# Layer gather in the second order: the table's part for a batch is copied to a fixed place by GpSimd

## The chip, the cores and the metric

The kernel runs on one core of a Trainium2 chip. The metric is the device time of one execution in microseconds; several executions give a median.

## What is computed

Four graph layers over 12500 nodes of 128 features and 200000 edges, each with layer norm before and a residual after. Two of their steps matter here, one of layer 2 and one of layer 3:

```python
# layer 2, the second of its two sums over edges
agg_bwd = jax.ops.segment_sum(w[:, None] * x[row], col, num_segments=n)
# layer 3
msg = edge_attr[:, None] * node[src]
ssum = jax.ops.segment_sum(msg, dst, num_segments=n)
```

Both need, for every edge, the row of a table of nodes that the edge's source names, and both add these rows up by the edge's target. The other steps (layer 0's multilayer net, layer 1's attention, layer 2's other sum, the sorting of the edges by source) are not touched by the change.

## The kernel before

The kernel is a row of phases (the loop at line 2767), with a barrier of all engines between any two. `p_lists` to `p_post` sort the edges and write lists; `p_l0` to `p_l1_nodes` are the first two layers; `p_l2f`, `p_l2b`, `p_l2_nodes`, `p_l3`, `p_l3_nodes` are the last two.

The edges stand in two orders. The first goes by target. The second goes by source: the table's 12500 rows are cut into 98 windows of 128, and the edges into NBQ = 558 batches of 512 places each, such that all places of a batch take rows of one window. `produce_q(table)` (line 2309) writes, for each batch, the 512 rows of the table to `xbuf`; `aggregate` then gathers from `xbuf` in the first order and sums. `produce_q` is called twice, by `p_l2b` (table t3d) and by `p_l3` (table t4d). `produce_p` (line 2429) is its sister for the other direction: 482 batches, four to a piece of the table, which GpSimd splits into three parts (lines 2478 to 2484 and 2520) at fixed places. It is not changed.

In `produce_q` the engines share a batch b like this:

- Before the batches, ScalarE (line 2365) and VectorE (line 2386) turn the whole table, in groups of four windows, into three bfloat16 parts whose sum is the float32 value. They lie in `TAB`, 384 elements (3 parts of 128) a window. The semaphore `pc[2]` says that all groups are there.
- ScalarE fetches the list `rowsqd` (which row of the window each place takes), half a round of six batches at a time (line 2353).
- TensorE spreads a batch's 512 row numbers to all 128 partitions with one product into PSUM bank s % 3 (line 2405, `kb`). It does so for batch b + 2 ahead of the products of batch b.
- VectorE compares them with the partition's number: 0 and 1 in bfloat16, 128x512 (line 2395, `oh`), in one of three places.
- TensorE makes 12 products (line 2419): four blocks of 128 places by three parts, summed in PSUM bank 3 + s % 3 (`gm`). The part of the table is read at `TAB` from an address in a register.
- ScalarE copies the bank to one of six places of `OUT` (line 2373, `ev`), and SyncE stores it to `xbuf`, 256 KB (line 2343).

The batches run in rounds of UN = 6: the first and the last round are written out, the 91 between them are a loop on each engine (`peeled`, line 2292). NITQ = 93 is the number of rounds. At the head of every round TensorE's queue loads the addresses of the round's six windows from the tile `RNG` (row 96) into registers, by `ranges` (line 153). `p_bases` (line 709) had written them as the window's number times 384. `past` (line 2303) is the wait that keeps a writer from a place still in use; in a loop it computes the semaphore's value in a register.

Of the kernel before, what the change touches and what calls it, by code (L numbers as in the profile page):

```python
# [5 lines left out]
I32 = mybir.dt.int32  # L6
U32 = mybir.dt.uint32
BF16 = mybir.dt.bfloat16
ALU = mybir.AluOpType
# [4 lines left out]
BE = 512  # L14
TP = 80
UN = 6
# [8 lines left out]
def gnn(nc, x, src, dst, ea, ew, u, W1, b1, W2, b2, w, w_r, att, loop_w, Ws, bs, Wd, bd_,  # L25
# [22 lines left out]
    NITQ = (((NE + 3 * NCK * NW) // 4 + 127 * NW + 127) // 128 + UN - 1) // UN  # L48
    NBQ = NITQ * UN
# [22 lines left out]
    NC = max(NN + 132, 12632)  # L72
    AREA = sb("AREA", [128, 3 * NC])
# [8 lines left out]
    RNG = sb("RNG", [128, max(2 * NR, 8 * NCK, 2 * NBQ) + 2], I32)  # L82
# [70 lines left out]
    def ranges(e, part, col, n, top_=None):  # L153
        return nc.values_load_multi_w_load_instructions(
            RNG[32 * part:32 * part + 1, bass.ds(col, n)], engines=[e.engine], min_val=0, max_val=top_ or NN + 1,
            skip_runtime_bounds_check_because="keys are node numbers")[1]
# [484 lines left out]
    def p_bases():  # L641

        p = Phase()
        n = NCK
        LOWF, IOX = p.tile([128, 128]), p.tile([128, NBQ])
# [19 lines left out]
        @p.on("vector")  # L665
        def _(e):
            link = chain(e, dv)
            e.wait_ge(ld, 16)
            e.wait_ge(g, 3)
            link(e.memset(ONS[:], 1.0))  # L670
            link(e.tensor_tensor_scan(LBI[0:n], ONS[0:n], NGR[0:n], 0.0, ALU.mult, ALU.add))
            e.memset(LBG[:, 98:99], -1.0)
            link(e.tensor_tensor(LBG[0:n, 0:98], LBI[0:n], NGR[0:n], ALU.subtract))
            e.wait_ge(mm, 2)
            link(e.tensor_scalar(CTI[:], PS[:, 4, 0:98], 127.0, None, ALU.add))
            e.tensor_copy(PRE[0:n], PS[0:n, 5, 0:98])
            link(e.tensor_scalar(CTI[:], CTI[:], 7, None, ALU.arith_shift_right))
            link(e.tensor_copy(TB[:], CTI[:]))
            link(e.tensor_tensor_scan(TBI[:], ONS[:], TB[:], 0.0, ALU.mult, ALU.add))
            link(e.tensor_tensor(TB[:], TBI[:], TB[:], ALU.subtract))  # L680
            link(e.scalar_tensor_tensor(out=DQ[0:n], in0=TB[0:n], scalar=128.0, in1=PRE[0:n], op0=ALU.mult, op1=ALU.add))
            link(e.tensor_tensor(DQ[0:n], DQ[0:n], LBG[0:n, 0:98], ALU.subtract))
            e.tensor_copy(DD[0:n, 0:1], DQ[0:n, 0:1])
            e.tensor_copy(DD[0:n, 98:99], DQ[0:n, 97:98])
            link(e.tensor_tensor(DD[0:n, 1:98], DQ[0:n, 1:98], DQ[0:n, 0:97], ALU.subtract))
            e.nop().then_inc(mm, 1)
            e.wait_ge(mm, 4)
            e.tensor_scalar(LBT[0:99, :], PS[0:99, 4, 0:n], -1.0, 0.5, ALU.mult, ALU.add)
            e.tensor_copy(TBT[0:98], PS[0:98, 6, 0:1])
            link(e.tensor_copy(DT[0:99], PS[0:99, 5, 0:n]))  # L690
            d3 = DD3.rearrange("p (k t) -> p t k", t=3) if (3 * NCK) % 2 == 0 else DD3[:, 0:3 * NCK].rearrange("p (k t) -> p t k", t=3)
            link(e.tensor_copy(d3[0:99, 0, :], DT[0:99]))
            link(e.tensor_tensor(DR[0][0:99], DT[0:99], d3[0:99, 0, :], ALU.subtract))
            link(e.tensor_copy(d3[0:99, 1, :], DR[0][0:99]))
            link(e.tensor_tensor(DR[1][0:99], DR[0][0:99], d3[0:99, 1, :], ALU.subtract))
            e.tensor_copy(d3[0:99, 2, :], DR[1][0:99])
            link(e.tensor_scalar(WG[0:98], IOX[0:98], TBT[0:98, 0:1], None, ALU.is_ge))
            e.nop().then_inc(mm, 1)
            e.wait_ge(mm, 6)


            for q in range(0, NBQ, 512):
                m = min(512, NBQ - q)
                i = e.tensor_scalar(IOX[:, q:q + m], PS[:, 6 + q // 512, 0:m], float(NW - 1), None, ALU.min)
            link(i)
            o = RNG[64:65, 0:2 * NBQ].rearrange("o (b t) -> o b t", t=2)
            e.tensor_scalar(o[:, :, 0], IOX[64:65, :], 128.0, None, ALU.mult)
            e.tensor_scalar(o[:, :, 1], IOX[64:65, :], 128.0, 1.0, ALU.mult, ALU.add)
            link(e.tensor_scalar(RNG[96:97, 0:NBQ], IOX[96:97, :], 384.0, None, ALU.mult))

        @p.on("tensor")
        def _(e):
# [1579 lines left out]
    def peeled(e, nb, un, f):  # L2292

        n = nb // un
        for b in range(un):
            f(b, b, 0)
        with e.Fori(1, n - 1) as it:
            for s in range(un):
                f(it * un + s, s, it)
        for b in range(un * (n - 1), nb):  # L2300
            f(b, b % un, b // un)

    def past(e, sem, b, back, each=1):

        n = b + 1 - back
        if not isinstance(n, int) or n > 0:
            e.wait_ge(sem, n * each)

    def produce_q(table):


        p = Phase()
        A0 = NC
        TAB = AREA[:, A0:A0 + 192 * 98].bitcast(BF16)
# [4 lines left out]

        RWZ = AREA[:, A0:A0 + UN * BE // 2]  # L2320
        RW = RWZ.bitcast(BF16).rearrange("o (s k) -> o s k", s=UN)
        OUT = [GF[:, 512 * s:512 * s + 512] for s in range(UN)]
        STG = [XR[:, 512 * i:512 * i + 512].rearrange("n (w f) -> n w f", w=4) for i in range(4)]
        groups = [(w_, min(4, NW - w_)) for w_ in range(0, NW, 4)]
        tl, fr = [p.sem(f"tl{i}") for i in range(4)], p.sem("fr")
        pc, sb_ = [p.sem(f"pc{i}") for i in range(3)], [p.sem(f"sb{i}") for i in range(2)]
        ra, rb, kb, oh, gm, ev, rz = (p.sem(k) for k in ("ra", "rb", "kb", "oh", "gm", "ev", "rz"))
# [5 lines left out]
        @p.on("sync")  # L2333
        def _(e):
            for k, (w_, m) in enumerate(groups):
                if k >= 4:
                    e.wait_ge(pc[2], k - 3)
                e.dma_start(STG[k % 4][:, 0:m, :], table[128 * w_:128 * (w_ + m), :].rearrange("(w n) f -> n w f", n=128)
                            ).then_inc(tl[k % 4], 16)

            def step(b, s, it):
                e.wait_ge(ev, b + 1)
                e.dma_start(xv[bass.ds(b, 1)].rearrange("b p k -> (b p) k"), OUT[s]).then_inc(st[s], 16)
            peeled(e, NBQ, UN, step)
            for s in range(UN):
                e.wait_ge(st[s], 16 * NITQ)

        @p.on("scalar")
        def _(e):
# [26 lines left out]
                    rows(it + 1, s // H)  # L2376
            peeled(e, NBQ, UN, step)

        @p.on("vector")
        def _(e):  # L2380
            def rest(k, i):
                if 0 <= k < len(groups):
                    w_, m = groups[k]
                    e.wait_ge(pc[i], k + 1)
                    v = STG[k % 4][:, 0:m, :]
                    e.tensor_tensor(v, v, tv[:, w_:w_ + m, i, :], ALU.subtract).then_inc(sb_[i], 1)
            e.memset(RWZ, 0.0).then_inc(rz, 1)
            for k in range(len(groups) + 1):
                rest(k, 0)
                rest(k - 1, 1)  # L2390

            def step(b, s, it):
                e.wait_ge(kb, b + 1)
                past(e, gm, b, 3)
                e.tensor_scalar(OHT[s % 3], PS[:, s % 3, :], IP[:, 0:1], None, ALU.is_equal).then_inc(oh, 1)  # L2395
            peeled(e, NBQ, UN, step)

        @p.on("tensor")
        def _(e):
            e.wait_ge(pc[2], len(groups))  # L2400

            def spread(b, s, it):
                e.wait_ge((ra, rb)[s // H], it * 16 + 16)
                past(e, oh, b, 3)
                e.matmul(PS[:, s % 3, :], ONB[:], RW[:, s, :], start=True, stop=True).then_inc(kb, 1)  # L2405
            held = {}

            def step(b, s, it):
                if s == 0:
                    held[0] = ranges(e, 3, it * UN, UN, 384 * 97)  # L2410
                if s + 2 < UN:
                    spread(b + 2, s + 2, it)
                elif not (isinstance(it, int) and it == NITQ - 1):
                    spread(b + 2, s + 2 - UN, it + 1)
                e.wait_ge(oh, b + 1)
                past(e, ev, b, 3)
                for r in range(4):
                    for k in range(3):
                        i = e.matmul(PS[:, 3 + s % 3, 128 * r:128 * r + 128], OHT[s % 3][:, 128 * r:128 * r + 128],  # L2419
                                     TAB[:, bass.ds(held[0][s] + 128 * k, 128)], start=(k == 0), stop=(k == 2))  # L2420
                i.then_inc(gm, 1)
            spread(0, 0, 0)
            spread(1, 1, 0)
            peeled(e, NBQ, UN, step)
# [371 lines left out]
```

## Time and profile before

| what | value |
| --- | --- |
| median of 3 runs | 9346.08 us |
| lowest, highest | 9331.73, 9353.26 us |
| the profiled execution's own time | 9342.07 us |
| its span | 9340.4 us |
| mean granted TensorE clock | 0.881 |
| PE busy | 7261.6 us (78%) |
| VectorE (DVE) busy | 6413.4 us (69%) |
| GpSimd (POOL) busy | 4037.3 us (43%) |
| ScalarE (ACT) busy | 3252.4 us (35%) |

PE is TensorE's matmul, PEld its weight load, SP is SyncE; a q behind an engine's name is its sequencer. Times stand in microseconds from the start of the span unless marked ns. A row of instructions gives the source line, the engine, the operation, what it writes and reads, how many there are, and their shortest, median and longest duration in ns. A row of the timeline gives the start, the length and then the instructions merged in it; in brackets is how long the engine had been idle, and what ended that. "issue" is time in which the engine waited for nothing that the profile shows. Granted clock is a share of TensorE's full speed, which is 2.4 GHz.

### The profile page before, as it was taken

The numbers are of one execution on the slowest core, as the hardware profiler recorded it, in microseconds if no ns is written. First come the engines' busy times: TensorE is split into PE (matmuls) and PEld (weight loads), VectorE is DVE, ScalarE is ACT, GpSimd is POOL, SyncE is SP. The second block draws the span as 40 slices with busy tenths as digits, with TensorE's granted clock in tenths as the row PEclk, the third lists the DMA queues.
The fourth block names the chain that finished last, engine by engine and source line by source line (L and its number), as shares of the span: only waits on it lengthen the run. The fifth ranks groups of instructions, "written<-read, shape, count | busy, mean of one in ns | idle before, by whom it ended". The sixth has DMA issues, their size and how long they took to land. (4 is left out here: it accounts for less than half of the span.)

```text
span 9340.4 us, 229910 instructions
## 1 busy us (share of the span) xinstructions
PE 7261.6 (78%) x60542; PEld 5838.2 (63%) x60851; DVE 6413.4 (69%) x20871; ACT 3252.4 (35%) x9379; POOL 4037.3 (43%) x4385
## 2 busy tenths in 40 slices
PE   4855677899968888888868977758877775886777
PEld 4855566544446666666667766646666664666665
DVE  5999888511167777777777766656666676666667
ACT  3533322222223333333235500025520025557882
POOL 2000577000057777777625567730037740006771
PEclk7975789999977777777789999989999988999997
DMA  0000466300024444444347866665556644556663
GB/s 21 2 2 1 110 140 140 91 24 24 23 73 105 107 105 106 106 105 105 91 147 271 289 183 191 191 156 230 230 199 191 192 156 178 230 230 183 184 182 106
DMA packets 645062, 1262.07 MB, mean 135 GB/s; under 512 B 126526, under 2 KB 183433, under 8 KB 644569
## 3 DMA queue, kind: packets, MB, share of 16 engines
q1 hardware_dynamic: 424337, 704.50, 23.0%
q0 software_dynamic: 199040, 544.46, 21.7%
q10 hardware_dynamic: 21452, 10.20, 0.4%
q8 instruction: 124, 2.03, 0.1%
q14 instruction: 109, 0.89, 0.0%
HBM read 780.96 MB, written 477.75 MB: 135 GB/s over the span
## 5 line engine op out<-in xcount | busy, mean ns | idle before, releaser
L1063 PE MATMUL PS<-w,GS 128*128 128x128 f32 x12176 | 1641.7, 284 | 499.9 <-DVE AREA L1008 224.2
L1063 PEld LDWEIGHTS PS<-w,GS 128*128 128x128 f32 x12176 | 1459.6, 192 | 682.3 <-DVE w L967 437.6
L1188 POOL DMA_INDIRECT GS<-xbuf,KI x964 | 1031.2, 1070 | 1759.7 <-ACTq L132 710.1
L1171 POOL DMA_INDIRECT GS<-t1d,KI x1564 | 1493.6, 955 | 488.0 <-issue 459.6
L2395 DVE TENSOR_SCALAR AREA<-PS,IP 128x512 bf16<-128x512 f32 x1116 | 837.7, 751 | 439.6 <-PE PS L2405 361.1
L967 DVE TENSOR_TENSOR w<-IO,KI 128x512 f32<-128x512 f32 (+1 forms) x1355 | 808.6, 597 | 424.6 <-issue 413.4
L2419 PE MATMUL PS<-AREA 128*128 x13392 | 961.1, 220 | 11.1 <-ACT GS L2373 1.4
L2419 PEld LDWEIGHTS PS<-AREA 128*128 128x128 bf16 x13392 | 843.8, 98 | 170.2 <-issue 49.2
L2373 ACT ACTIVATE GS<-PS 128x512 f32<-128x512 f32 x1116 | 666.3, 597 | 613.8 <-PE PS L2419 613.5
L1188 POOL DMA_INDIRECT GS<-pbuf,XR x558 | 595.3, 1067 | 209.4 <-issue 101.4
L1598 ACT ACTIVATE w<-PS,w 128x48 f32<-128x48 f32 x1564 | 341.7, 301 | 926.9 <-PE PS L1593 926.9
L1126 ACT ACTIVATE GS<-GS,XR 128x128 f32<-128x128 f32 x1928 | 603.6, 389 | 106.0 <-DMA GS<-xbuf,KI 98.3
L1063 PE MATMUL PS<-w,XR 128*128 128x128 f32 x3128 | 510.7, 313 | 165.8 <-DVE w L967 162.3
L2405 PE MATMUL PS<-AREA,ONB 128*128 128x512 bf16 x928 | 353.2, 381 | 340.2 <-issue 143.1
L1650 PE MATMUL PS<-w,XR 128*128 128x128 f32 x3128 | 586.2, 345 | 0.0
L1063 PEld LDWEIGHTS PS<-w,XR 128*128 128x128 f32 x3128 | 430.8, 214 | 205.9 <-DVE w L967 197.1
L1207 POOL DMA_INDIRECT keyd<-AREA x482 | 480.0, 996 | 178.8 <-issue 146.1
L1644 PE MATMUL PS<-w,GS 128*128 128x128 f32 x3128 | 543.2, 332 | 0.0
L1650 PEld LDWEIGHTS PS<-w,XR 128*128 128x128 f32 x3128 | 500.3, 244 | 49.2 <-issue 28.6
L1008 DVE TENSOR_TENSOR AREA<-AREA,PS 128x128 f32 (+1 forms) x1921 | 515.9, 269 | 18.0
L967 DVE TENSOR_TENSOR w<-IO,XR 128x512 f32<-128x512 f32 x558 | 388.6, 696 | 192.5 <-issue 188.3
L1644 PEld LDWEIGHTS PS<-w,GS 128*128 128x128 f32 x3128 | 514.8, 248 | 0.5
(410 smaller groups left out, 12508.2 us busy)
## 6 DMA issues: line engine op xcount, KB each, us to landing
xbuf<-GS SPq DMA_DIRECT2D x1116, 256.0 KB
XR<-in_edge_attr SPq DMA_DIRECT2D x780, 256.0 KB
pbuf<-AREA SPq DMA_DIRECT2D x482, 256.0 KB
GS<-t1d,KI POOLq DMA_INDIRECT x1564
GS<-xbuf,KI POOLq DMA_INDIRECT x964
GS<-pbuf,XR POOLq DMA_INDIRECT x558
AREA<-t2d ACTq DMA_DIRECT2D x121, 64.0 KB
keyd<-AREA POOLq DMA_INDIRECT x482
```

The costliest lines, as they stand in the source:

```text
L967: return e.tensor_tensor(SEL[s % 3], IO[:, 0:width].unsqueeze(1).to_broadcast([128, 4, width]), kl.unsqueeze(2).to_broadcast([128, 4, widt ...
L1008: i = e.tensor_tensor(ACC[:, bass.ds(wv, width)], ACC[:, bass.ds(wv, width)], PS[:, q, 0:width], ALU.add).then_inc(acc, 1)
L1063: i = e.matmul(PS[:, s % 3, 0:128], feats(s)[0:m, r, 0:D], SELW[s % 3][0:m, width * r:width * r + 128], start=(r == 0), stop=(r == 3))
L1126: i = e.activation(feats(s)[:, r, :], feats(s)[:, r, :], ACT.Copy, scale=weight[:, bass.ds(b * 4 + r, 1)])
L1171: e.indirect_dma_start(GS[0:m, s, r, 0:wide], None, table, bass.IndirectOffsetOnAxis(ap=idx[0:m, c:c + 1].bitcast(U32), axis=0)).then_inc( ...
L1188: e.indirect_dma_start(GF[:, 512 * s:512 * s + 512], None, buf, bass.IndirectOffsetOnAxis(ap=idx[:, b:b + 1].bitcast(U32), axis=0)).then_i ...
L1207: e.indirect_dma_start(keyd, bass.IndirectOffsetOnAxis(ap=SI[:, b:b + 1].bitcast(U32), axis=0), MP[:, 5 * b:5 * b + 5], None).then_inc(sc[ ...
L1644: n = e.matmul(PS[:, 4 + i, 0:128], GS[0:m, s, r, 0:D], LLW[l][0:m, WD * r:WD * r + 128], start=(r == 0), stop=(r == 3))
L1650: n = e.matmul(PS[:, 4 + i, 128:256], EA[0:m, s, r, :], LLW[l][0:m, WD * r:WD * r + 128], start=(r == 0), stop=(r == 3))
L2373: e.activation(OUT[s], PS[:, 3 + s % 3, :], ACT.Copy).then_inc(ev, 1)
L2395: e.tensor_scalar(OHT[s % 3], PS[:, s % 3, :], IP[:, 0:1], None, ALU.is_equal).then_inc(oh, 1)
L2419: i = e.matmul(PS[:, 3 + s % 3, 128 * r:128 * r + 128], OHT[s % 3][:, 128 * r:128 * r + 128], TAB[:, bass.ds(held[0][s] + 128 * k, 128)], ...
```

## The change

In `produce_q`, TensorE no longer reads `TAB` at an address from a register. GpSimd, which had nothing to do in these stages, copies the 384 bfloat16 elements of the batch's window to one of six fixed places `WT`, as an integer addition of zero on 192 words of 32 bits; TensorE waits for the copy (`wt`) and reads there. GpSimd waits until the products of six batches earlier are done (`gm`), and loads the addresses of 18 batches at once, in a loop of 18 batches. The addresses are in words of 32 bits now, so the factor in `p_bases` is 192.

```diff
-            link(e.tensor_scalar(RNG[96:97, 0:NBQ], IOX[96:97, :], 384.0, None, ALU.mult))
+            link(e.tensor_scalar(RNG[96:97, 0:NBQ], IOX[96:97, :], 192.0, None, ALU.mult))
...
+        A0 += UN * BE // 2
+
+        WTI = [AREA[:, A0 + 192 * i:A0 + 192 * i + 192].bitcast(I32) for i in range(UN)]
+        WT = [AREA[:, A0 + 192 * i:A0 + 192 * i + 192].bitcast(BF16) for i in range(UN)]
+        TABI = AREA[:, NC:NC + 192 * 98].bitcast(I32)
+        assert A0 + 192 * UN <= 3 * NC and NITQ % 3 == 0
+        ZI = p.tile([128, 1], I32)
+        wt, zi = p.sem("wt"), p.sem("zi")
...
+        @p.on("gpsimd")
+        def _(e):
+
+            e.memset(ZI[:], 0).then_inc(zi, 1)
+            e.wait_ge(zi, 1)
+            e.wait_ge(pc[2], len(groups))
+            held = {}
+
+            def step(b, s, it):
+                if s == 0:
+                    held[0] = ranges(e, 3, it * (3 * UN), 3 * UN, 192 * 97)
+                past(e, gm, b, UN)
+                e.tensor_tensor(WTI[s % UN], TABI[:, bass.ds(held[0][s], 192)], ZI[:, 0:1].to_broadcast([128, 192]),
+                                ALU.add).then_inc(wt, 1)
+            peeled(e, NBQ, 3 * UN, step)
...
-            held = {}
 
             def step(b, s, it):
-                if s == 0:
-                    held[0] = ranges(e, 3, it * UN, UN, 384 * 97)
                 if s + 2 < UN:
                     spread(b + 2, s + 2, it)
                 elif not (isinstance(it, int) and it == NITQ - 1):
                     spread(b + 2, s + 2 - UN, it + 1)
                 e.wait_ge(oh, b + 1)
+                e.wait_ge(wt, b + 1)
                 past(e, ev, b, 3)
                 for r in range(4):
                     for k in range(3):
                         i = e.matmul(PS[:, 3 + s % 3, 128 * r:128 * r + 128], OHT[s % 3][:, 128 * r:128 * r + 128],
-                                     TAB[:, bass.ds(held[0][s] + 128 * k, 128)], start=(k == 0), stop=(k == 2))
+                                     WT[s][:, 128 * k:128 * k + 128], start=(k == 0), stop=(k == 2))
```

## Rows read from the trace of the kernel before

**Rows 1.** Windows: length, busy us of PE, PEld, DVE, ACT, POOL; PEclk, DMA share, GB/s.

```profile
6254.00:6892.00 638.00, 530.27 (x7159) 437.05 (x7251) 418.32 (x558) 332.47 (x557) 0.00 (x0) 1.00 0.59 229
7789.00:8428.00 639.00, 531.21 (x7160) 437.42 (x7252) 418.79 (x558) 332.76 (x558) 0.00 (x0) 1.00 0.59 229
```

**Rows 2.** Who waited for whom, 6254 to 6892: us in total, times, longest.

```profile
ACT GS L2373 <- PE PS L2419: 306.7, 556, 3.1
DVE AREA L2395 <- PE PS L2405: 180.5, 277, 1.9
PEld PS L2405 <- issue: 115.9, 92, 1.9
```

**Rows 3.** Line 154, register loads on TensorE's sequencer, 6262 to 6889.

```profile
L154 PEldq TENSOR_LOAD <-RNG x92: 1040/1576/2093, 6260.7 to 6885.5; - x92
```

**Rows 4.** Timeline of one round, 6504.9 to 6511.

```profile
6505.83 0.10 PEld L2405 LDWEIGHTS PS<-AREA,ONB 128*128 128x128 bf16 x1
...
6506.71 0.10 PEld L2405 LDWEIGHTS PS<-AREA,ONB 128*128 128x128 bf16 x1
...
6507.60 0.10 PEld L2405 LDWEIGHTS PS<-AREA,ONB 128*128 128x128 bf16 x1
...
6508.74 0.60 ACT L2373 ACTIVATE GS<-PS 128x512 f32<-128x512 f32 x1 [0.29 <-PE PS L2419]
6510.23 0.10 PEld L2405 LDWEIGHTS PS<-AREA,ONB 128*128 128x128 bf16 x1 [1.70 <-issue]
```

**Rows 5.** Line 2405's weight loads, first stage, then second.

```profile
L2405 PEld LDWEIGHTS PS<-AREA,ONB x558: 95/98/151, 6252.9 to 6889.7; 128*128 128x128 bf16 x186
...
L2405 PEld LDWEIGHTS PS<-AREA,ONB x558: 95/98/151, 7788.3 to 8425.3; 128*128 128x128 bf16 x186
```

**Rows 6.** produce_p: weight loads in the timeline, then line 2614's waits, 4960 to 5370.

```profile
4952.10 0.10 PEld L2621 LDWEIGHTS PS<-AREA 128*128 128x128 bf16 x1
...
4952.99 0.10 PEld L2621 LDWEIGHTS PS<-AREA 128*128 128x128 bf16 x1
...
4953.88 0.10 PEld L2621 LDWEIGHTS PS<-AREA 128*128 128x128 bf16 x1
...
  POOL AREA L2520: 55.5, 150
```

**Rows 7.** Windows inside produce_p, columns as in rows 1.

```profile
4960.00:5060.00 100.00, 92.31 (x1310) 79.21 (x1335) 77.03 (x104) 55.39 (x103) 52.09 (x129) 1.00 0.82 288
```

**Rows 8.** GpSimd's additions: two of the timeline, then by line.

```profile
4940.04 0.42 POOL L2480 TENSOR_TENSOR AREA<-AREA 128x128 f32<-128x128 f32 x1
4940.54 0.40 POOL L2482 TENSOR_TENSOR AREA<-AREA,w 128x128 bf16<-128x128 f32 x1
...
L2478 POOL TENSOR_TENSOR AREA<-AREA,w x121: 397/398/400, 4909.0 to 5379.3; 128x128 bf16<-128x128 f32 x121
...
L2480 POOL TENSOR_TENSOR AREA<-AREA x121: 425/427/432, 4909.5 to 5379.8; 128x128 f32<-128x128 f32 x121
...
L2238 POOL TENSOR_TENSOR KI<-XR,RDEG x25: 1029/1036/1197, 4676.0 to 4867.6; 128x512 f32<-128x512 f32 x24, 53x512 f32<-53x512 f32 x1
```

**Rows 9.** Register loads elsewhere: GpSimd's one (line 2459), VectorE's, 7000 to 7600.

```profile
L2459 POOLq TENSOR_LOAD <-w x1: 504/504/504, 4906.0 to 4906.0; - x1
...
L154 DVEq TENSOR_LOAD <-RNG x71: 540/849/871, 7001.7 to 7569.0; - x71
```

**Rows 10.** Timeline of the first stage's beginning.

```profile
6252.86 0.13 PEld L2405 LDWEIGHTS PS<-AREA,ONB 128*128 128x128 bf16 x2 [59.43 <-ACT AREA L2365]
...
6254.40 1.24 PEld L2419 LDWEIGHTS PS<-AREA 128*128 128x128 bf16 x12 [0.57 <-issue]
```

**Rows 11.** VectorE's comparison in produce_p: by line, then two in the timeline.

```profile
L2583 DVE TENSOR_SCALAR AREA<-PS,IP x482: 740/751/753, 4909.6 to 5381.3; 128x512 bf16<-128x512 f32 x161
...
4945.91 1.55 DVE L2583 TENSOR_SCALAR AREA<-PS,IP 128x512 bf16<-128x512 f32 x2
```

**Rows 12.** VectorE's comparison in both stages of produce_q.

```profile
L2395 DVE TENSOR_SCALAR AREA<-PS,IP x1116: 740/751/752, 6253.5 to 8425.8; 128x512 bf16<-128x512 f32 x186
```

## The prediction

> **What bounds the kernel now.** I read the stages first. Line 2419's products and line 2405's spreads run in two stretches only, one for each call of produce_q, 6254 to 6892 us and 7789 to 8428 us [rows 1, 5], 638 us each; the rest of the kernel holds none of the edited lines and I leave it alone. In these two stretches no engine is full: PE is busy 83% of the time, VectorE 66%, ScalarE 52%, GpSimd not at all, the transfer engines 0.59 of the time, and PE's granted clock is 1.00, the 2.4 GHz level [rows 1]. So the next thing to read is who waits, and on what: ScalarE and VectorE wait for PE (307 and 181 us), while PE's weight loads wait 116 us for "issue", that is for nothing that the profile shows, in 92 pieces [rows 2]. 92 is one less than the 93 rounds of six batches. The same count has the register load: 92 TENSOR_LOADs of 1.04 to 2.09 us on PE's sequencer [rows 3].
>
> The order in time shows it as a picture [rows 4]. Inside a round the weights of a batch's spread begin to load at 6505.83, 6506.71 and 6507.60: 0.886 us apart (two pitches in 1.77). Then the next one begins at 6510.23, 2.63 us later, with 1.70 us of "issue" before it. PE's sequencer reaches the head of the loop, asks for six addresses, and nothing is sent to the array until they have come. One stage takes (6889.7 - 6252.9)/557 = 1.1433 us a batch by its first and last spread, the other (8425.3 - 7788.3)/557 = 1.1436 [rows 5], against 0.886 within a round: 0.257 us a batch, or 1.54 us a round. The stage is bound by PE plus this hole in it.
>
> **What the change removes.** The load of the registers and the 46 ns address instructions (three a batch) leave PE. Without the hole PE should hold 0.886 us. Does the loop's end cost anything by itself? The trace answers: lines 2621 and 2614 make the same one-hot products, 12 and a spread, with no register load on PE. Line 2621's weight loads begin at 4952.10, 4952.99 and 4953.88 [rows 6], 0.89 and 0.89 us apart, in a stage whose PE loop ends every eight batches; the PE busy share there is 92% at a granted clock of 1.00 [rows 7]. Its remaining idle time is put to GpSimd, 55.5 us in 150 waits [rows 6]. So a denser PE keeps its clock, and 0.886 can be held.
> The saving is 636.8 - 557 x 0.886 = 143.3 us in the first stage and 637.0 - 493.5 = 143.5 us in the second, 286.8 us together.
>
> **What it adds: a GpSimd copy for each batch.** 1116 integer additions of 128x192, of a broadcast zero, and one load of 18 registers for 18 batches. No such form is in the trace, so I bound it. Below: the 128x128 additions of produce_p, 0.40 us with a broadcast operand and 0.43 with two full ones [rows 8]. Above: the 128x512 addition at 1.036 us [rows 8]. The slope between 427 ns and 1036 ns is 1.59 ns an element, which gives 0.43 + 64 x 0.00159 = 0.53 us. I take 0.53, since 192 lies nearest to the 128 row; whether integers cost GpSimd more no row says, and the end at 1.04 stays in the range. Between two additions stand 0.08 us (starts at 4940.04 and 4940.54 for 0.42 of work [rows 8]). The load: one value took GpSimd 0.50 us [rows 9]; VectorE's loads, of two or twelve values, took 0.54 at the least and 0.85 in the middle [rows 9], near 0.03 us a value, so 18 take 1.0 to 1.1. With branch and the last copy under way I put 1.5 us, with 2.1 as the upper end from PE's slowest. Per batch: 0.53 + 0.08 + 1.5/18 = 0.69 us, under PE's 0.886. The work is hidden by PE. The hole at the end of 18 is hidden too: six places let GpSimd be up to six batches ahead, and five finished ones give PE 5 x 0.886 = 4.4 us to live on. If the cover were gone (a copy above 0.72 us), GpSimd would set the pace at once.
>
> The Trainium skill, page "Runtime: NRT & Kernel Launch", section "Instruction fetch mechanics", puts a register load at about 200 ns a register. An estimate by it: 18 x 0.2 = 3.6 us a load, GpSimd at 0.81 us a batch in place of 0.69, still below PE, though a copy of 0.61 us would then be enough to make it the bound. The twelve-value loads of 0.85 us in this trace don't agree with it, and the sum goes by them.
>
> **What it adds as waits.** PE waits for `wt` before each batch's products. Behind that wait stand the following spreads, so a late copy would also starve VectorE; at 0.69 against 0.886 it isn't late after the first batch. At the start of a stage GpSimd loads (1.1) and copies (0.53) after the table is complete. Before, PE's first product came 1.54 us after its first spread (6252.86 and 6254.40) [rows 10]; now 1.6 or a little more: 0.2 us each, below the rounding. GpSimd waits for `gm`, six batches back; nothing is queued behind it but copies. The factor 192 for 384 in p_bases costs nothing, same instruction. The zeroing of ZI is one tiny GpSimd instruction while it is idle.
>
> **What is late next.** VectorE's comparison, 0.751 us, can follow itself at 0.80 (two in 1.55 us) [rows 11], under 0.886. ScalarE's copy takes 0.60 [rows 4]. The stores: 262144 bytes in 0.886 us are 296 GB/s; produce_p moves 288 with engines at 0.82 of the time [rows 7]. If 288 were the most, a batch would take 0.91 us and the gain be 260 us; this sets the upper end of the main case. None of them binds first.
>
> **Sum.** 9342.07 (the profiled execution, span 9340.4) - 286.8 + 0.4 = 9055.7. The median of the three runs, 9346.08, is 4 above the profiled one, so I say 9060.
>
> **Rivals.**
> Main case, PE holds 0.886 in both stages: 9060, its own range 9040 to 9085. Chance 0.80.
> GpSimd becomes the pace, though still better than before. It needs a copy of 0.73 to 0.98 us (0.886 and 1.143 less 0.16 for gap and load). For it: integers have no row. Against: 128x128 at 0.40 [rows 8]. With a copy at 0.85 the pace is 1.01, gain 1116 x 0.133 = 148: about 9200. Chance 0.10.
> GpSimd becomes the pace and the kernel slower. The same place, the copy before each batch's products, from 0.98 us on. Priced with the 512-element row, 1.04 + 0.16 = 1.20 us a batch: 1116 x 0.057 = +64, 9410. Against it: a third of those elements. Chance 0.03.
> GpSimd and VectorE exclude each other. If a comparison could not run beside a copy, a batch would take 0.751 + 0.53 = 1.28 us: 1116 x 0.138 = +154, 9500. Against: in produce_p, with GpSimd busy 52% [rows 7], VectorE's comparison of this very form takes 740/751/753 ns [rows 11] and 740/751/752 where GpSimd is silent [rows 12], and GpSimd's additions vary by 3 ns [rows 8]. Chance 0.03.
> The Trainium skill, page "SBUF — State Buffer", section "SBUF: two separate sides", speaks of such a lock: the pair of ports that VectorE and GpSimd share goes to one instruction whole, and the other blocks, for a VectorE operation in a two-port mode or with two SBUF inputs. Would it hold here, the 9500 above is the time; the comparison reads PSUM, so the rule itself exempts it, and the rows agree.
> The hole stays. If the 2.6 us came from the branch and the round's end and not from the load, nothing is won: 9346. Against: line 2621's unbroken pitch [rows 6] and loads as many as holes [rows 2, 3]. Chance 0.04.
>
> **How the numbers follow.** A measurement of this kernel tells about 0.2% from no change, 19 us. Faster by more: main and the first rival, 0.90. Within: the hole stays, 0.04. Slower: 0.06. The range starts at 9035 (a pitch of 0.87, with the run spread) and goes to 9140 (a pitch of 0.955, into the first rival, copy near 0.80); what is left out is its dearer part and the three others, under 2 in 10.
>
> **What would show it.** Right: line 2405's weight loads 0.886 us apart through all rounds, x558 in 494 us; no register load on PE in these stages; both stages some 495 us long; VectorE near 85% busy, transfers near 0.77 and 296 GB/s; copies of about 0.53 us on GpSimd. ScalarE's waits for PE fall from 307 us to around 160. Wrong: PE's idle time put to the GpSimd copy; copies above 0.72 us; VectorE's comparison or the copies much longer than alone; granted clock under 1.00; or pitch kept at 0.886 with holes remaining every six batches. If the stages lose 143 us each and the total doesn't, something outside of them moved.

## The result, and the profile after

The changed kernel takes 9121.03 us in the median of four runs (9113.24 to 9125.56), the kernel before 9343.43 beside it (9331.73 to 9353.26): ratio 0.9762, 95% interval 0.9745 to 0.9778. It is faster by 222 us, inside the range; 9060 had been said, 283 under the kernel before by these runs. So a good fifth of the gain is missing, 61 us, and the study asks where it stayed.

The two stages have shrunk. Windows of both, with the columns of [rows 1]:

```profile
6244.00:6780.00 536.00, 501.46 (x7254) 430.88 (x7254) 418.96 (x559) 333.90 (x560) 273.62 (x558) 0.99 0.71 274
...
7673.00:8200.00 527.00, 500.62 (x7254) 430.18 (x7254) 418.72 (x558) 333.62 (x560) 274.19 (x558) 0.99 0.72 278
```

They are 102 and 112 us shorter than in [rows 1], where 143 each was the sum. More exact are the spreads (line 2429 now, against [rows 5]), first stage and then second:

```profile
L2429 PEld LDWEIGHTS PS<-AREA,ONB x558: 97/98/152, 6244.8 to 6775.6; 128*128 128x128 bf16 x186
...
L2429 PEld LDWEIGHTS PS<-AREA,ONB x558: 97/98/151, 7673.5 to 8196.3; 128*128 128x128 bf16 x186
```

(6775.6 - 6244.8)/557 = 0.953 us a batch, and 0.939 in the second, not 0.886. From first to last the stages are 106.0 and 114.2 us shorter, 220 of the 225 between the two profiled spans (9340.4 and 9115.2). The excess over 0.886 is 557 x (0.067 + 0.053) = 67 us; 5 of them lie in the slower beginnings, since pad20 below, without holes, has an excess of 5 as well. Now the copy, the load of registers and VectorE's comparison, by line:

```profile
L2399 POOL TENSOR_TENSOR AREA<-AREA,w x1116: 493/504/507, 6246.7 to 8194.0; 128x192 int32<-128x192 int32 x186
...
L154 POOLq TENSOR_LOAD <-RNG x62: 1532/2119/6195, 6244.8 to 8178.2; - x62
...
L2419 DVE TENSOR_SCALAR AREA<-PS,IP x1116: 743/751/752, 6245.4 to 8196.8; 128x512 bf16<-128x512 f32 x186
```

The copy is 0.504 us, close to the 0.53 of the prediction. The comparison is what it was in [rows 12] although GpSimd now works beside it. The load isn't what was reckoned: 1.0 to 1.1 had been put, 2.1 is the median and 6.2 the longest. Who waited for whom, 6245 to 6780, against [rows 2]:

```profile
ACT GS L2381 <- PE PS L2441: 200.6, 556, 4.1
POOL AREA L2399 <- PE PS L2441: 159.3, 344, 2.3
POOL AREA L2399 <- issue: 150.7, 16, 58.4
...
PEld PS L2441 <- issue: 36.7, 19, 2.4
PE PS L2441 <- POOL AREA L2399: 31.8, 16, 2.1
```

TensorE waits 16 times for a copy, 2.0 us each, and GpSimd stands 16 times at "issue" before a copy: once for 58.4 us at the stage's start, and 15 times for 6.2 us. There are 31 loads in a stage, so only every second one shows. The loads one by one bear this out, three that follow each other:

```profile
L154 POOLq TENSOR_LOAD <-RNG x1: 5951/5951/5951, 6294.4 to 6294.4; - x1
L154 POOLq TENSOR_LOAD <-RNG x1: 2111/2111/2111, 6314.3 to 6314.3; - x1
L154 POOLq TENSOR_LOAD <-RNG x1: 5942/5942/5942, 6330.2 to 6330.2; - x1
```

It goes on so, by turns, to the end. What a long one does, in the order of time:

```profile
6294.05 0.50 POOL L2399 TENSOR_TENSOR AREA<-AREA,w 128x192 int32<-128x192 int32 x1 [0.38 <-PE PS L2441]
...
6298.97 0.10 PEld L2429 LDWEIGHTS PS<-AREA,ONB 128*128 128x128 bf16 x1
...
6300.73 1.89 POOL L2399 TENSOR_TENSOR AREA<-AREA,w 128x192 int32<-128x192 int32 x4 [6.17 <-issue]
...
6301.46 0.67 PEld L2441 LDWEIGHTS PS<-AREA 128*128 128x128 bf16 x12 [2.40 <-issue]
...
6302.09 0.10 PEld L2429 LDWEIGHTS PS<-AREA,ONB 128*128 128x128 bf16 x1
```

GpSimd's last copy is at 6294.05, its next at 6300.73. TensorE uses up the five places that lie ready, stands before its products from about 6299, and starts with them when the first new copy is done. Two spreads that should be 0.89 apart are 3.12 apart (6298.97 and 6302.09). In the second stage the long loads take 5.61 us and leave 1.72.

### The profile page after: what moved, and what is told of

The parts are those of the page before. It is cut to its first block and busy times, and to the rows that moved or that the text cites. A ratio compares the mean times of both kernels' runs of the same rounds, so it can differ in the third digit from the quotient of the medians.

```text
span 9115.2 us, 230332 instructions
## 1 busy us (share of the span) xinstructions
PE 7221.3 (79%) x60850; PEld 5827.1 (64%) x60851; DVE 6414.1 (70%) x20871; ACT 3251.0 (36%) x9379; POOL 4580.0 (50%) x5503
## 5 line engine op out<-in xcount | busy, mean ns | idle before, releaser
L1063 PEld LDWEIGHTS PS<-w,GS 128*128 128x128 f32 x12176 | 1457.8, 192 | 678.9 <-DVE w L967 444.5
L2441 PE MATMUL PS<-AREA 128*128 128x128 bf16 x13392 | 934.7, 220 | 56.4 <-POOL AREA L2399 56.4
L2399 POOL TENSOR_TENSOR AREA<-AREA,w 128x192 int32<-128x192 int32 x1116 | 547.8, 504 | 615.7 <-PE PS L2441 330.2
L2429 PE MATMUL PS<-AREA,ONB 128*128 128x512 bf16 x1116 | 425.4, 382 | 137.2 <-ACT AREA L2373 137.2
```

Of the source, the lines that this page charges most:

```text
L1063: i = e.matmul(PS[:, s % 3, 0:128], feats(s)[0:m, r, 0:D], SELW[s % 3][0:m, width * r:width * r + 128], start=(r == 0), stop=(r == 3))
L2399: e.tensor_tensor(WTI[s % UN], TABI[:, bass.ds(held[0][s], 192)], ZI[:, 0:1].to_broadcast([128, 192]), ALU.add).then_inc(wt, 1)
```

## Experiments

Why does every second load take three times as long? The list has one word of 4 bytes for a batch, so the loads of 18 begin 72 bytes apart: every second one begins 8 bytes past a multiple of 16. The kernel before had the same alternation on TensorE, unseen in the prediction: its loads of six, 24 bytes apart, took 1.1 us in even rounds and 2.0 in odd ones, behind one median of 1576 ns in [rows 3]. Two of them that follow each other:

```profile
L154 PEldq TENSOR_LOAD <-RNG x1: 1991/1991/1991, 6508.0 to 6508.0; - x1
L154 PEldq TENSOR_LOAD <-RNG x1: 1142/1142/1142, 6515.3 to 6515.3; - x1
```

Theory: where a load begins sets its time. Rival: a long load leaves GpSimd behind, and that makes the next one short, by turns.

**pad20: every load of 18 begins at a multiple of 16 bytes.**

```diff
-            link(e.tensor_scalar(RNG[96:97, 0:NBQ], IOX[96:97, :], 192.0, None, ALU.mult))
+            q3 = RNG[96:97, 0:0 + 20 * (NBQ // 18)].rearrange("o (g t) -> o g t", t=20)
+            link(e.tensor_scalar(q3[:, :, 0:18], IOX[96:97, :].rearrange("o (g t) -> o g t", t=18), 192.0, None, ALU.mult))
...
-                    held[0] = ranges(e, 3, it * (3 * UN), 3 * UN, 192 * 97)
+                    held[0] = ranges(e, 3, it * 20, 3 * UN, 192 * 97)
```

> The changed kernel, but the addresses of 18 batches lie 20 words apart in the list, so that every one of GpSimd's loads of 18 registers begins at a multiple of 16 bytes (72 bytes apart before: every second one began 8 bytes past such a multiple). Theory (where a load begins sets its time; the changed kernel's loads of 5.6 to 6.0 us are the ones that begin 8 bytes off): all 62 loads take about 2.0 to 2.1 us, TensorE never waits for a copy, the spreads are 0.886 us apart all through, and the 61 us of holes go: 9121 - 61 = 9060 us. Rival (a slow load leaves GpSimd behind, and that makes the next one quick, by turns, wherever they begin): loads still 5.9 and 2.1 by turns, 9121 us.

9068.7 us (five runs) against 9355.02 of the kernel before beside it: ratio 0.9695 (0.9682 to 0.9708), 286.3 us less. The prediction's sum was 286.8 for the holes. By first and last spread the two stages are 281.8 us shorter (496.0 each); the other 4 lie within the interval, so that the two numbers agree to half a microsecond is luck. Loads, then TensorE's one remaining wait for a copy in the first stage, then the stage's window:

```profile
L154 POOLq TENSOR_LOAD <-RNG x62: 1537/1990/2120, 6247.4 to 8122.3; - x62
...
PE PS L2442 <- POOL AREA L2400: 1.2, 1, 1.2
...
6251.00:6743.00 492.00, 487.11 (x7107) 426.32 (x7198) 415.16 (x554) 330.50 (x554) 274.40 (x555) 1.00 0.77 295
```

No load is above 2.12 us, TensorE waits for a copy once (1.2 us), and the transfers run at 295 GB/s. The mean pitch is 0.8905 us by first and last spread, 0.886 from one to the next after the first few. The 61 us are back. It beats both kernels. The alternation is gone, so the rival is out.

**pad20off8: every load begins 8 bytes past a multiple.**

```diff
+            q3 = RNG[96:97, 2:2 + 20 * (NBQ // 18)].rearrange("o (g t) -> o g t", t=20)
...
+                    held[0] = ranges(e, 3, it * 20 + 2, 3 * UN, 192 * 97)
```

> As pad20, but the list begins two words later, so that every load begins 8 bytes past a multiple of 16. Theory: all loads of the loop take 5.6 to 6.0 us, and TensorE has a hole of 1.7 to 2.2 us every 18 batches where the changed kernel has it every 36: 61 us more than the changed kernel, 9180 us. Rival (by turns): 9121 us.

9224.19 us, ratio 0.9865 (0.985 to 0.988). With the data, the order and the number of loads of pad20, only 8 bytes further on, they take:

```profile
L154 POOLq TENSOR_LOAD <-RNG x62: 4048/5630/6496, 6249.2 to 8277.0; - x62
```

5.96 us in the first stage and 5.61 in the second, in every round but the first two of each. So the place where a load begins sets its time. The size of the loss was off: 155 us over pad20, where 122 was forecast. Windows of the first stage, the second, three stretches around one hole of the first, and the 4.1 us behind another of its holes, which ends at 6367.9:

```profile
6256.00:6840.00 584.00, 515.00 (x7089) 445.91 (x7181) 414.39 (x553) 329.62 (x553) 269.71 (x553) 0.95 0.64 248
7752.00:8296.00 544.00, 491.75 (x7097) 424.76 (x7188) 414.89 (x553) 329.75 (x553) 268.27 (x553) 1.00 0.69 267
6500.50:6502.60 2.10, 0.84 (x13) 0.78 (x14) 0.00 (x0) 0.00 (x0) 1.58 (x4) 1.00 0.51 198
6502.60:6506.70 4.10, 3.88 (x39) 3.48 (x38) 2.08 (x3) 1.79 (x3) 2.66 (x6) 0.58 0.33 129
6506.70:6515.00 8.30, 8.25 (x123) 7.12 (x122) 6.92 (x10) 5.38 (x10) 4.54 (x9) 1.00 0.69 267
6368.70:6372.80 4.10, 4.05 (x62) 3.53 (x61) 3.16 (x5) 2.86 (x5) 3.50 (x8) 1.00 0.49 191
```

Behind the hole that ends at 6501.8 the granted clock is 0.58 for 4.1 us, that is mostly at the lower level of 1.2 GHz, and 1.00 after them; behind the other one, as long, it stays at 1.00. It falls behind 17 of the first stage's 30 holes of some 2.2 us, and the spreads behind such a hole lose 1.6 us more. In the second stage, with holes of 1.7 us, it falls behind none of the 30. The spreads give the whole account: the holes cost 119 us, the falls of the clock 27, and the longer first loads 5. That is 152 us over pad20; the medians say 155. The forecast of 122 had left out the clock.

**before_pad8: the same cure for the kernel before.**

```diff
-            link(e.tensor_scalar(RNG[96:97, 0:NBQ], IOX[96:97, :], 384.0, None, ALU.mult))
+            q3 = RNG[96:97, 0:0 + 8 * (NBQ // 6)].rearrange("o (g t) -> o g t", t=8)
+            link(e.tensor_scalar(q3[:, :, 0:6], IOX[96:97, :].rearrange("o (g t) -> o g t", t=6), 384.0, None, ALU.mult))
...
-                    held[0] = ranges(e, 3, it * UN, UN, 384 * 97)
+                    held[0] = ranges(e, 3, it * 8, UN, 384 * 97)
```

> The kernel before, with TensorE's own loads of six registers, but the list has 8 words a round, so that every load begins at a multiple of 16 bytes. In the kernel before the loads took 1.1 us in the even rounds and 2.0 us in the odd ones, which began 8 bytes off. Theory: all loads 1.1 us, the odd rounds' holes shrink by 0.87 us, 93 times over both stages: 81 us less than the kernel before, 9262 us. Rival (by turns): 9343 us, no change.

9272.24 us, ratio 0.991 (0.9895 to 0.9926), 83 us less than the kernel before, as the theory has it. TensorE's loads in the first stage, against [rows 3]:

```profile
L154 PEldq TENSOR_LOAD <-RNG x92: 1022/1111/1257, 6269.0 to 6852.5; - x92
```

**six: GpSimd loads six registers at a time, list as it was.**

```diff
-                    held[0] = ranges(e, 3, it * (3 * UN), 3 * UN, 192 * 97)
+                    held[0] = ranges(e, 3, it * UN, UN, 192 * 97)
...
-            peeled(e, NBQ, 3 * UN, step)
+            peeled(e, NBQ, UN, step)
```

> The changed kernel, but GpSimd loads the addresses of six batches at a time (rounds of 6 in place of 18, the list as it is, 24 bytes apart, every second load 8 bytes off). Theory: a load's time goes with the number of registers and where it begins, some 1.1 us even and 2.0 us odd as on TensorE before; GpSimd's mean is 0.50 + 1.7/6 or so = 0.79 us a batch, still under 0.886, and each load is shorter than the 4.4 us that five finished places cover. TensorE has no hole: 9060 us. If GpSimd's loads of six take over 2.6 us in the mean, it sets the pace and the time goes above 9060 by 1116 us for each us a batch.

9070.51 us, ratio 0.97 (0.9687 to 0.9713). All loads of both stages:

```profile
L154 POOLq TENSOR_LOAD <-RNG x186: 802/1080/1909, 6252.3 to 8137.3; - x186
```

They alternate, 1.02 and 1.85 us, and none reaches what the places cover. Nothing is lost (pad20 took 9068.7): what hurt was not the number of misplaced loads but that one of them was longer than the cover.

**load20: two registers more, an aligned 20.**

```diff
-                    held[0] = ranges(e, 3, it * 20, 3 * UN, 192 * 97)
+                    held[0] = ranges(e, 3, it * 20, 20, 192 * 97)
```

> pad20, but GpSimd loads 20 registers at a time, and uses 18. Theory (a load makes one access of about 0.33 us for each whole, aligned 16 bytes and one for each single word besides: 18 words from an aligned start are 4 + 2 = 6 accesses, 1.98 us; 18 from 8 bytes off are 18 accesses, 5.6 to 5.9): 20 aligned words are 5 accesses, so the load is shorter by one access, about 1.65 us, though it brings two registers more. Rival (an aligned load costs by the register, 0.11 us each): 2.2 us. The time stays that of pad20, 286 us under the kernel before, since the load is covered either way.

One run: 9047.38 us, 284 under its kernel before (9331.69). What the run is read for is not its time but the loads:

```profile
L154 POOLq TENSOR_LOAD <-RNG x62: 1322/1786/1914, 6245.1 to 8117.5; - x62
```

1.91 us in the first stage and 1.75 in the second, where 18 took 2.11 and 1.98. Two registers more make it 0.2 us shorter: the rival by the register is out. A whole access of 0.33 was forecast to go, and 0.2 went, so the size of an access isn't the same throughout.

**before_load8: TensorE loads an aligned eight.**

```diff
-                    held[0] = ranges(e, 3, it * 8, UN, 384 * 97)
+                    held[0] = ranges(e, 3, it * 8, 8, 384 * 97)
```

> before_pad8, but TensorE loads 8 registers a round and uses 6. Theory by accesses: 2 in place of 3, so a load is 0.3 us shorter, 186 holes shrink by that, and the time is some 56 us under before_pad8, 139 under the kernel before. Rival (by the register): loads 0.1 to 0.2 us longer, 20 to 40 us over before_pad8.

9169.56 us, ratio 0.9827 (0.9814 to 0.9841), 162 under the kernel before, that is 79 more than before_pad8 gained; 139 and 56 were forecast. The loads of the first stage:

```profile
L154 PEldq TENSOR_LOAD <-RNG x92: 598/662/846, 6261.4 to 6804.2; - x92
```

0.66 us against 1.11 with six registers. They are 0.45 us shorter, not 0.3, and 186 x 0.45 = 84 us accounts for the gain. The same exchange, one sixteen-byte piece for two single words, saved only 0.2 us on GpSimd (load20); why is open. More than half of the whole gain could thus be had without GpSimd's copies, by the place and length of the loads alone. The rest is about what the loads of 0.66 us still cost on TensorE, 186 x 0.66 = 123 us. The change takes them away by moving them to GpSimd; whether TensorE could hide them by itself, by asking for a round's addresses earlier, was not tried.

**three: three places in place of six.**

```diff
-                past(e, gm, b, UN)
-                e.tensor_tensor(WTI[s % UN], TABI[:, bass.ds(held[0][s], 192)], ZI[:, 0:1].to_broadcast([128, 192]),
+                past(e, gm, b, 3)
+                e.tensor_tensor(WTI[s % 3], TABI[:, bass.ds(held[0][s], 192)], ZI[:, 0:1].to_broadcast([128, 192]),
...
-                                     WT[s][:, 128 * k:128 * k + 128], start=(k == 0), stop=(k == 2))
+                                     WT[s % 3][:, 128 * k:128 * k + 128], start=(k == 0), stop=(k == 2))
```

> pad20 with three places for the copies in place of six: GpSimd can be three batches ahead, not six. Theory (a load is covered by the batches that lie ready, and what is left of it is TensorE's hole; in the changed kernel 5.95 us left 2.22 and 5.61 left 1.72, so six places cover 3.7 to 3.9): three places cover 3 x 0.886 = 2.66 less, 1.1 to 1.2 us, and a load of 1.98 to 2.11 leaves 0.8 to 1.0 us, every 18 batches: 60 holes, 53 us, so 233 under the kernel before. If the number of places did not matter at these loads: 286 under it.

9108.82 us against 9331.69, ratio 0.9762 (0.9748 to 0.9775), 223 less (233 forecast). The hole in the order of time:

```profile
6426.76 0.10 PEld L2430 LDWEIGHTS PS<-AREA,ONB 128*128 128x128 bf16 x1
...
6427.65 0.10 PEld L2430 LDWEIGHTS PS<-AREA,ONB 128*128 128x128 bf16 x1
...
6427.90 0.60 ACT L2382 ACTIVATE GS<-PS 128x512 f32<-128x512 f32 x1 [0.29 <-PE PS L2442]
6428.20 1.43 POOL L2400 TENSOR_TENSOR AREA<-AREA,w 128x192 int32<-128x192 int32 x3 [2.31 <-PE PS L2442]
6428.93 0.67 PEld L2442 LDWEIGHTS PS<-AREA 128*128 128x128 bf16 x12 [1.19 <-ACT GS L2382]
...
6429.56 0.10 PEld L2430 LDWEIGHTS PS<-AREA,ONB 128*128 128x128 bf16 x1
```

A load of 2.1 us, fully hidden with six places, leaves 1.0 us with three (6427.65 to 6429.56, less 0.89). The row puts the wait down to ScalarE, whose copy was done at 6428.5; the first of GpSimd's three ended some 0.2 us later, just ahead of the products. By first and last spread the two stages lose 53.7 us against pad20, where 53 was forecast; the medians differ by 10 more.

**twice: each copy made twice.**

```diff
+        WDI = [AREA[:, A0 + 192 * i:A0 + 192 * i + 192].bitcast(I32) for i in range(UN, 2 * UN)]
...
+                e.tensor_tensor(WDI[s % UN], TABI[:, bass.ds(held[0][s], 192)], ZI[:, 0:1].to_broadcast([128, 192]),
+                                ALU.add).then_inc(wt, 1)
...
-                e.wait_ge(wt, b + 1)
+                e.wait_ge(wt, b * 2 + 2)
```

> pad20, but GpSimd makes each copy twice (once to places that nobody reads). The copies follow each other at 0.462 us when nothing holds them, so a batch takes GpSimd 2 x 0.462 = 0.924 and the load (2.84 - 0.46)/18 = 0.13 more: 1.06 us, over TensorE's 0.886. Theory (from there GpSimd sets the pace): 1116 x 0.17 = 194 us over pad20, some 92 under the kernel before, still faster since 1.143 is the point of return; TensorE waits for the copy in nearly every batch. VectorE's comparison stays at 0.751 us though GpSimd is busy nearly all the time.

9097.85 us against 9331.69, ratio 0.9751 (0.9738 to 0.9765): 234 less than the kernel before, where 92 was forecast. The window inside the first stage, then VectorE's comparison:

```profile
6250.00:6750.00 500.00, 495.20 (x6967) 400.06 (x7055) 407.71 (x543) 324.08 (x544) 500.00 (x1083) 1.00 0.74 285
...
L2423 DVE TENSOR_SCALAR AREA<-PS,IP x1116: 742/751/753, 6242.7 to 8173.1; 128x512 bf16<-128x512 f32 x186
```

GpSimd is busy 500 of 500 us with 1083 copies, 0.462 each, 0.924 a batch: it sets the pace, as the theory has it. Against their own kernels before, pad20 gains 286 us and twice 234: 52 us between them, and 40 by first and last spread (516.0 against 496.0 in each stage), where the copies alone give 1116 x (0.924 - 0.886) = 42. So the load costs next to nothing. One of the loads, and the first copy that uses its registers:

```profile
L154 POOLq TENSOR_LOAD <-RNG x1: 1998/1998/1998, 6323.1 to 6323.1; - x1
...
6327.22 0.50 POOL L2401 TENSOR_TENSOR AREA<-AREA,w 128x192 int32<-128x192 int32 x1
```

The load runs from 6323.1 to 6325.1 while GpSimd makes copies of the round before, and four more of these follow before the first that needs it. When GpSimd is behind, its sequencer is thus some copies ahead of the engine and fetches the registers while they run. In pad20, where GpSimd is ahead and its sequencer stands at the wait for the place, the load begins late and GpSimd stands still for it (2.8 us from one copy to the next); and just there it is covered by what lies ready. The term "load/18" of the prediction's GpSimd budget was wrong for the case in which it would have mattered.

## Why the prediction was right, and where it was off

- **The stage is bound by PE and a hole at the register load.** Right. pad20, with the loads off TensorE and quick, has a pitch of 0.886 and gains 281.8 us in the two stages, 286.3 by the medians; the sum was 286.8. That the loop's end costs nothing by itself, read from line 2621 in [rows 6], holds.
- **The copy: 0.53 us.** 0.504. Following one another, copies stand 0.462 apart, so the 0.08 between two of them was too much.
- **The load of 18 registers: 1.0 to 1.1 us, 1.5 with what lies around it, 2.1 at most.** This step failed. It measured 2.0 to 2.1 in one half of the rounds and 5.6 to 6.0 in the other. The line was drawn from VectorE's loads of two and twelve in [rows 9], 0.03 us a register. But the loads of twelve lie 48 bytes apart, never misplaced, and are three whole pieces of sixteen bytes. The row that was nearer, TensorE's own loads of six in [rows 3], was read only as a longest of 2.09 us, and its spread from 1.04 not asked about; its two levels by turns were in the trace of before. A longest load of six was thus taken as the upper end for eighteen.
- **The range, 9035 to 9140.** That it held is luck. The main case had 9040 to 9085 of its own, and 9121 is outside of that. The stretch above 9085 was there for a dear copy, near 0.80 us; the copy took 0.504, and what filled the stretch was the long load, for which the prediction had no rival. Of its own signs of being wrong two came: TensorE's idle time put to the copy (31.8 us in the first stage), and a granted clock under 1.00 (0.99). Transfers ran at 274 and 278 GB/s, not 296.
- **Five finished places cover 4.4 us.** The kind was right, the size a little high: a load of 5.95 left a hole of 2.2 and one of 5.61 left 1.7, so the cover is 3.7 to 3.9. The first stage's 15 holes come to 33.2 us and the second's 15 to 26.3, and one fall of the clock to 1.6: 61 us, the whole gap between 9060 and 9121.
- **200 ns a register**, the estimate by the Trainium skill ("Runtime: NRT & Kernel Launch", section "Instruction fetch mechanics"), was set aside for the twelve in 0.85. Neither is a rule here: this kernel's loads took from 0.07 us a register (twelve, aligned) to 0.33 (eighteen, misplaced). The estimate's 3.6 us is near the mean of a stage's loads, 3.9 and 3.7, but no load took that long: they took 2.0 to 2.1 or 5.6 to 6.0.
- **Waits.** PE does not wait for `wt` except behind a long load: right, in kind. ScalarE's waits for PE fell from 307 to 201 us, and to 165 in pad20, where 160 was said.
- **The rival of the shared ports** is out: the comparison takes 751 ns with GpSimd idle, half busy, and busy all the time (twice). The Trainium skill's exemption of such an operation ("SBUF — State Buffer", section "SBUF: two separate sides") agrees with these rows.
- **The rivals of a dear copy.** Their condition (0.73 us) did not occur. Made to occur by twice, 0.924 a batch, the pace was GpSimd's. The limit was too low, though: since the load is hidden when GpSimd is behind, GpSimd sets the pace when copies follow each other at more than 0.886 us, not from a copy of 0.73 on.
- **Stores at 296 GB/s** are no bound: 295 in pad20.

## What to carry to other kernels

A load of registers from a list is priced by its place before its length: begin it at a multiple of 16 bytes and take a multiple of four words, padding the list if need be. Here that alone, with the loads still on TensorE, was worth 162 us, where the whole change with an aligned list gained 286. When a step is moved to an idle engine, price its longest instance against the cover (here one place less than there are, times the pitch, less 0.5 to 0.7 us: with six places 3.7 to 3.9 us, with three 1.1 to 1.2), not its mean against the pitch; and look at a group's spread by turns, even and odd, before using its median.

## What the runs showed of the hardware

- Register loads, as medians: six aligned words 1.0 us on GpSimd and 1.1 on TensorE, six from 8 bytes off 1.85 and 2.0; eighteen aligned 2.0 to 2.1, from 8 bytes off 5.6 to 6.0; twenty aligned 1.75 to 1.9; eight aligned 0.66 on TensorE; twelve aligned 0.85 on VectorE. This fits one access of 0.3 to 0.4 us for each whole, aligned sixteen bytes and for each single word besides, better than a price by the register, if from a start 8 bytes off every word counts as a single one (18 accesses in 5.6 to 6.0 us, 6 in 1.85 to 2.0). The accesses themselves were not seen, and other offsets than 8 bytes were not tried. Starts at any multiple of 16 (pad20's are 80 bytes apart) are alike.
- The same load takes 5.96 us in the first stage and 5.61 in the second, and 2.11 and 1.98 when aligned. In twice it is the other way round, 1.98 and 2.08. Why the stages differ is open.
- A hole of 2.2 us in a dense stream of products can lower the granted clock over the next 4 us: in pad20off8's first stage it fell behind 17 of 30 such holes, to 0.58 in the one shown above. It fell behind none of the 30 holes of 1.7 us in the second. In the changed kernel's first stage it fell behind one hole of 15, and not behind the next:

```profile
6301.40:6305.50 4.10, 4.03 (x40) 3.37 (x41) 1.50 (x2) 1.45 (x3) 3.18 (x8) 0.66 0.27 106
6337.50:6341.50 4.00, 4.00 (x63) 3.53 (x61) 2.70 (x4) 2.39 (x4) 3.68 (x8) 1.00 0.35 135
```

  What decides between such holes stays open.
- An integer addition of 128x192 words takes GpSimd 0.504 us alone and 0.462 in a row, no more than the 0.53 that the prediction drew from the float additions of [rows 8].
